# An exponential written in place over the transposed scores in PSUM, in a cross-attention kernel

## The reference, cut to what matters

```python
q = _split_heads(hidden_states @ w_q, HEADS)
out_text = _merge_heads(_sdpa(q, k, v))                      # softmax over 146 text keys
out_ip = _merge_heads(_sdpa(q, k_ip, v_ip, mask=mask_ip))    # softmax over 8 image keys
out = (out_text + IP_SCALE * out_ip) @ w_out + b_out + residual
```

## Time and profile before

| | |
|---|---|
| time, median of 3 runs | 802.34 us (801.8 to 805.32) |
| span of the profiled execution | 801.8 us, as long as the lowest of the runs; no other time is given for it |
| busy TensorE / VectorE / ScalarE / GpSimd | 91% / 71% / 36% / 30% |
| mean granted clock of TensorE | 0.981 |

### The profile page before, as it was taken

The page is one execution under the profiler, slowest core; times in us unless marked ns, Lnnn a source line. Parts: engine busy times, 40 slices in busy tenths (PEclk is TensorE's granted clock), DMA queues, the critical chain, the costliest instruction groups (busy, mean ns, idle before and its releaser), DMA issues.

```text
span 801.8 us, 19010 instructions
## 1 busy us (share of the span) xinstructions
PE 732.8 (91%) x6384; PEld 645.1 (80%) x6384; DVE 565.4 (71%) x1694; ACT 287.3 (36%) x615; POOL 237.1 (30%) x347
## 2 busy tenths in 40 slices
PE   5968979999999999999999899999999999999887
PEld 4755458888888898989898888888898989898766
DVE  3241287778786968687878777786968686878774
ACT  1111026253443525151616152443525151616051
POOL 1000143324150606042423324150606051423334
PEclk9969999999999999999999999999999999999979
DMA  9989714344343525342424344343525342423220
GB/s 257 268 242 220 168 26 109 93 109 112 98 106 86 133 77 129 92 116 80 126 80 118 86 117 108 99 106 85 133 77 131 89 119 80 126 80 93 76 67 34
DMA packets 85115, 91.27 MB, mean 114 GB/s; under 512 B 10768, under 2 KB 69776, under 8 KB 85068
## 3 DMA queue, kind: packets, MB, share of 16 engines
q1 hardware_dynamic: 85084, 90.87, 43.6%
HBM read 40.42 MB, written 10.62 MB: 64 GB/s over the span
## 4 chain that ended last, share of the span: by engine, by line
PE 59%; DVE 18%; SPq 9%; issue 7%; DMA 7%; ACT 1%; DVEq 0%; ACTq 0%
PE psum L864 30%; PE psum L913 7%; PE psum L958 4%; SPq L407 4%; PE psum L939 4%; DVE p_lo L730 4%; PE psum L944 3%; DMA q_stack<-aux_a 3%; DVE o_parts L745 3%; DVE inv_den L737 2%; PE psum L835 2%; DMA q_stack<-mask_scratch 2%; DVE neg_max L706 2%; PE psum L982 2%; PE psum L799 2%
## 5 line engine op out<-in xcount | busy, mean ns | idle before, releaser
L450 POOL TENSOR_TENSOR attn<-o_parts 128x128 f32<-128x128 f32 x160 | 72.9, 456 | 443.0 <-DVE o_parts L742 443.0
L706 DVE TENSOR_REDUCE neg_max<-psum 128x2 f32<-128x292 f32 x320 | 144.1, 451 | 18.0 <-PE psum L913 14.8
L864 PE MATMUL psum<-wo_both,at_hi 128*128 128x320 f32 x640 | 154.1, 313 | 0.0
L730 DVE TENSOR_TENSOR p_lo<-p_whole,p_hi 128x512 f16<-128x512 f32 x160 | 137.1, 857 | 2.4 <-ACT p_hi L553 0.9
L913 PE MATMUL psum<-k_stack,q_stack 104*128 104x154 f32 x640 | 108.5, 284 | 20.0 <-DVE neg_max L707 13.4
L542 ACT ACTIVATE q_hi<-psum 128x256 fp32r<-128x256 f32 x80 | 30.7, 384 | 258.5 <-PE psum L864 258.5
L958 PE MATMUL psum<-v_tail,p_tail 128*128 128x264 f32 x320 | 105.5, 411 | 17.8 <-DVE p_lo L730 15.8
L864 PE MATMUL psum<-xt_hi,wq_hi 128*128 128x256 f32 x400 | 115.2, 288 | 1.0 <-DVE xt_lo L675 1.0
L913 PEld LDWEIGHTS psum<-k_stack,q_stack 104*128 104x128 f32 x640 | 89.6, 193 | 31.3 <-DVE neg_max L707 22.1
L864 PE MATMUL psum<-xt_lo,wq_hi 128*128 128x256 f32 x400 | 113.1, 283 | 0.0
L864 PE MATMUL psum<-xt_hi,wq_lo 128*128 128x256 f32 x400 | 113.0, 283 | 0.0
(11 more groups left out here) (87 smaller groups left out, 1331.4 us busy)
## 6 DMA issues: line engine op xcount, KB each, us to landing
q_stack<-q_hi SPq DMA_DIRECT2D x128, 96.0 KB
x_in<-in_x SPq DMA_DIRECT2D x16, 640.0 KB, 4.1
x_res<-in_x SPq DMA_DIRECT2D x16, 640.0 KB, 4.0
out<-out_sb SPq DMA_DIRECT2D x32, 320.0 KB
q_stack<-q_hi SPq DMA_DIRECT2D x128, 64.0 KB
q_stack<-q_lo SPq DMA_DIRECT2D x64, 96.0 KB
q_stack<-q_lo SPq DMA_DIRECT2D x64, 64.0 KB
q_stack<-aux_a SPq DMA_DIRECT2D x48, 64.0 KB, 2.3
```

What stands on the lines that cost most here:

```text
L450: nc.gpsimd.tensor_tensor(cols, o_parts[:, qt, 0:4, :], o_parts[:, qt, 4:8, :], ALU.add).then_inc(att_half, 1)
L706: nc.vector.tensor_reduce(dst[:, :, 0], src[:, :, 0:TEXT], AX_X, ALU.max, negate=True)
L730: nc.vector.tensor_tensor(p_lo[:, -g % P_SLOTS, 2 * u:2 * u + 2, :], p_whole[:, u, :, :], p_hi[:, -g % P_SLOTS, 2 * u:2 * u + 2, :], ALU.s ...
L864: last = nc.tensor.matmul(ps, l(c), r(c), start=(i == 0), stop=(i == len(terms) - 1))
```

## The change

The buffer `p_whole` goes. ScalarE writes `p_hi` first, and then the full-precision exponential over the scores themselves, in the PSUM bank that it reads. VectorE's split reads that bank. So the bank is in use until the split is done: TensorE's ST step for tile n now waits for the split of tile n-2, where that tile has one (u < 2), and for the exponential where it has none (u = 2). ScalarE's waits for the split go; at the first AT step TensorE waits for the last split. The order of steps on each engine stays as it was, the late place of the splits on VectorE too. In SBUF `at_hi_0` no longer shares its place with other buffers.

```diff
--- before.py
+++ after.py
@@ -227,13 +227,13 @@
         q_stack = sb("q_stack", [P, HEADS, QB], F32R)
         aux_rows = [sb("aux_a", [16 * len(SET_A), QB], F32R), sb("aux_b", [16 * len(SET_B), QB], F32R)]
         p_lo = sb("p_lo", [P, P_SLOTS, 4, QB], F16)
+        at_hi_0 = sb("at_hi_0", [P, QT, 4 * P], F32R)
         with ExitStack() as turns:
 
 
-            at_hi_0, at_lo_0 = (sb(f"at_{part}_0", [P, QT, 4 * P], F32R, turns) for part in ("hi", "lo"))
+            at_lo_0 = sb("at_lo_0", [P, QT, 4 * P], F32R, turns)
             at_hi_1, at_lo_1 = (sb(f"at_{part}_1", [P, QT, P], F32R, turns) for part in ("hi", "lo"))
-            at_hi, at_lo = (at_hi_0, at_hi_1), (at_lo_0, at_lo_1)
-        p_whole = sb("p_whole", [P, 2, 2, QB])
+        at_hi, at_lo = (at_hi_0, at_hi_1), (at_lo_0, at_lo_1)
         p_hi = sb("p_hi", [P, P_SLOTS, 4, QB], F16)
         p_tail = sb("p_tail", [P, P_SLOTS, QB])
         inv_den = sb("inv_den", [P, QT, 8])
@@ -546,20 +546,13 @@
                         act.wait_ge(st_ready, t * 15 - 15 + 3 * g + u + 1)
                         src = scores_t[(3 * g + u) % 2]
                         if u < 2:
-                            if g > 0:
-
-                                act.wait_ge(p_split, t * 10 - 10 + 2 * g + u - 1)
-                            nc.scalar.activation(p_whole[:, u, :, :].rearrange("p h q -> p (h q)"), src[:], ACT.Exp)
                             nc.scalar.activation(p_hi[:, -g % P_SLOTS, 2 * u:2 * u + 2, :].rearrange("p h q -> p (h q)"), src[:],
-                                                 ACT.Exp).then_inc(exp_done, 1)
+                                                 ACT.Exp)
+                            nc.scalar.activation(src[:], src[:], ACT.Exp).then_inc(exp_done, 1)
                         else:
                             nc.scalar.activation(p_tail[:, -g % P_SLOTS, :], src[:, 0:QB], ACT.Exp).then_inc(exp_done, 1)
                     if kind == "AT":
                         qt, u = args
-                        if (qt, u) == (0, 0):
-
-                            act.wait_ge(p_split, t * 10 + 0)
-
                         act.wait_ge(at_ready[u], t * 2 - 2 + qt + 1)
                         c0, c1 = AT_CHUNKS[u]
                         nc.scalar.activation(at_hi[u][:, qt, :], scores_t[u][:, 0:P * (c1 - c0)], ACT.Copy
@@ -727,7 +720,8 @@
                         g, u = args
 
                         dve.wait_ge(exp_done, t * 15 - 15 + 3 * g + u + 1)
-                        nc.vector.tensor_tensor(p_lo[:, -g % P_SLOTS, 2 * u:2 * u + 2, :], p_whole[:, u, :, :],
+                        nc.vector.tensor_tensor(p_lo[:, -g % P_SLOTS, 2 * u:2 * u + 2, :], 
+                                                scores_t[(3 * g + u) % 2][:].rearrange("p (h q) -> p h q", h=2),
                                                 p_hi[:, -g % P_SLOTS, 2 * u:2 * u + 2, :], ALU.subtract).then_inc(p_split, 1)
                     if kind == "PV":
                         g, qt = args
@@ -929,9 +923,13 @@
                             n = 0 if g in SET_A else 1
 
                             pe.wait_ge(aux_in[n], t * (16 * len((SET_A, SET_B)[n])))
-                        if g or u > 1:
-
-                            pe.wait_ge(exp_done, t * 15 - 15 + 3 * g + u - 1)
+                        before = 3 * g + u - 2
+                        if before >= 0 and before % 3 < 2:
+
+                            pe.wait_ge(p_split, t * 10 - 10 + 2 * (before // 3) + before % 3 + 1)
+                        elif before >= 0:
+
+                            pe.wait_ge(exp_done, t * 15 - 15 + before + 1)
                         ps = scores_t[(3 * g + u) % 2]
                         if u < 2:
                             for i in range(2):
@@ -972,6 +970,7 @@
                         if (qt, u) == (0, 0):
 
                             pe.wait_ge(exp_done, t * 15 + 0)
+                            pe.wait_ge(p_split, t * 10 + 0)
                         if qt > 0:
 
                             pe.wait_ge(al_done[u], t * 2 - 2 + qt)
```

## The result

The changed kernel takes 875.46 us (874.18 to 876.49, four runs) against 802.6 us: a ratio of 1.0894, with a 95% interval of 1.0869 to 1.0919. The forecast was 874. The profiled execution spans 872.4 us, 70.6 more than before, where 71.7 were forecast.

A forecast was written before the change was run, and what follows sets the result against it. TensorE's order of work was taken as the bound (busy 91% of 801.8 us). Fifteen blocks at 4.7 us (70.5), plus 3.5 for the BACK-only pass, less 2.3 of DMA waits, made 71.7: 874 us, range 858 to 892.

The forecast's parts named there:

- Durations: VectorE's split from PSUM taken as 0.68 us for all ten in a block, ScalarE's exponential into PSUM as 0.60.
- GpSimd still in the way: Rival: GpSimd still disturbs VectorE's split, which stays at 0.97 us; about 911 us in all, 3%.
- a dearer exponential: Rival: ScalarE's exponential in place takes 0.60 us more; 25 us in all, 880 to 900 us, 12%.
- The block: One full block, TensorE's new waits for splits less what is given back: 4.7 us more, 70.5 for fifteen blocks.
- the 0.2: Near a block's end, AT(0,1) on TensorE waits somewhat longer for `attn`: +0.2 us.
- The sum: Whole kernel: 70.5 + 3.5 - 2.3 = 71.7 us on a span of 801.8, median 0.5 higher: 874 us.
- the last pass: The one pass with BACK alone, no Q step between, partly at half clock: 3.5 us more, bounds 0 and 4.7.
- The three waits for DMAs in the blocks: TensorE's waits for mask-row DMAs before S(0,0) go, since S(0,0) starts 4.5 us later: -2.3 us.
- Faster: Rival: VectorE paces the PV steps, so 0.29 us less on six splits a block gives 786 us; 4%.
- The clock: Rival: TensorE's clock falls in the new waits, 3 us a block, 45 in all, about 920 us; 8%.
- the first rival: The rival of ScalarE's exponential in place costing 0.60 us more: 25 us in all, 900 at the upper bound, 12%.
- The same walk: Step-by-step reckoning of TensorE's waits along one block; with 0.60 us more per in-place exponential, 1.7 more a block.

The follow-up runs named there:

- experiment 4: The kernel before, with GpSimd's additions cut to one column of each head's 32, most attention output left out: 799.95 us, ratio 0.9949.
- experiment 2: The kernel before, SBUF buffer kept, but TensorE's ST steps and first AT step wait for the splits as in the changed kernel: 908.48 us, ratio 1.1301.
- experiment 10: The changed kernel plus a third exponential per tile on ScalarE, written to an unused fp16 buffer between the two: 903.09 us, ratio 1.1268.

## Why the prediction was right, point by point

TensorE's timeline in one block of the changed kernel; its S(4,1) starts at 598.17, that of the block in the earlier trace rows at 553.56, which sets the two side by side:

```profile
602.36 0.39 PE L937 MATMUL psum<-q_stack,k_stack 120*128 120x256 f32 x1 [0.88 <-DVE p_lo L723]
...
607.38 0.39 PE L937 MATMUL psum<-q_stack,k_stack 120*128 120x256 f32 x1 [1.00 <-DVE p_lo L723]
...
610.25 0.39 PE L942 MATMUL psum<-q_stack,k_tail 120*128 120x256 f32 x1 [0.44 <-DVE p_lo L723]
...
611.62 0.39 PE L937 MATMUL psum<-q_stack,k_stack 120*128 120x256 f32 x1 [0.63 <-DVE p_lo L723]
...
614.46 0.39 PE L942 MATMUL psum<-q_stack,k_tail 120*128 120x256 f32 x1 [0.45 <-DVE p_lo L723]
615.83 0.38 PE L937 MATMUL psum<-q_stack,k_stack 120*128 120x256 f32 x1
...
619.58 0.38 PE L942 MATMUL psum<-q_stack,k_tail 120*128 120x256 f32 x1 [1.29 <-DVE p_lo L723]
...
624.43 0.32 PE L907 MATMUL psum<-k_stack,q_stack 104*128 104x154 f32 x1
```

The brackets are the waits that the prediction put there, each behind VectorE's split, at six of the seven ST steps to which it gave a price; at the seventh, ST(4,0), it had only 0.1. The distances from step to step, before and after:

| from, to | before | after | grew | forecast |
|---|---|---|---|---|
| S(4,1), ST(1,0) | 3.02 | 4.19 | 1.17 | 1.2 |
| ST(1,0), ST(2,0) | 4.02 | 5.02 | 1.00 | 1.0 |
| ST(2,0), ST(2,2) | 2.42 | 2.87 | 0.45 | 0.4 |
| ST(2,2), ST(3,0) | 0.55 | 1.37 | 0.82 | 0.8 |
| ST(3,0), ST(3,2) | 2.76 | 2.84 | 0.08 | 0.06 |
| ST(3,2), ST(4,0) | 1.34 | 1.37 | 0.03 | 0.1 |
| ST(4,0), ST(4,2) | 2.28 | 3.75 | 1.47 | 1.4 |
| ST(4,2), S(0,0) | 5.24 | 4.85 | -0.39 | -0.4 |
| S(0,0) to the block's end | | | 0.00 | 0.2 |
| the block | 42.65 | 47.28 | 4.63 | 4.7 |

- *Durations.* The split at 0.68 held (681 ns), and so did the exponential at 0.60 (595). The rivals that hung on them, GpSimd still in the way and a dearer exponential, are out.
- *The block.* The table: every step within 0.1 us but the last, where AT(0,1) did not cost the 0.2. The prediction's own terms add up to 4.76, which it wrote as 4.7; by fifteen blocks that is 0.9 us.
- *The sum.* Fourteen distances between blocks grew by 63.3 us (4.5 each, the lost DMA waits already in it), the last pass by 3.0 (forecast 3.5), the setup by 0.3. The first distance grew by 4.0; it is 53.2 us long before, though the prediction took all fifteen for alike. In all 70.6. The three waits for DMAs in the blocks went, as forecast. In the last step there is some luck: the median stands 3.1 us above the profiled span and not 0.5, and the span is 1.1 us shorter than forecast, so two errors of opposite sign meet in the 874.
- *Faster.* Refuted twice: by the result, and by experiment 4, in which the shorter split alone gave 0.5% and not 2%, as a DMA wait took part of the place of the split's.
- *The clock.* The window from 600 to 620 has TensorE busy 15.32 of 20 us at a granted clock of 1.00. The new waits, 1.3 us at most in this block, did not bring the clock from 2.4 to 1.2 GHz. The prediction put TensorE's share from ST(2,0) to ST(4,2) at 70%; it was 77% (9.39 of 12.20 us). That the rival was worth its place shows in experiment 2: there the clock fell in six full blocks (in the one shown, after a stretch with TensorE busy 70%), for about 5 us in all, not the 45 of the rival.
- *The two rules of the Trainium skill.* That VectorE pays more for a source in PSUM ("VectorE: DVE Perf Modes", the section on the errata) is not borne out: 681 ns from PSUM, 0.69 us from SBUF undisturbed, and the sum without it was the closer one. That idleness takes TensorE's clock back ("TensorE: Matmul & The Clock Gate", Part 1, the HAM clock gate) did not come into play in the changed kernel (clock 1.00 in all fourteen full blocks); the traces of experiments 2 and 10, in which TensorE waits 90.5 and 89.1 us for splits instead of 76.2, agree with it, with 0.97 in six and in five blocks.
- *What the price of the first rival got wrong.* The same walk that gave 25 us for 0.60 us more on each tile gave 17 for 0.49, and experiment 10 measured 27.6. So the upper bound of 900 was too low, but hardly for the reason of too little cover: in blocks at full clock the walk was off by 0.1 to 0.3 us. It left out the clock, which fell in some blocks, and the first block and the last pass, which grew more than the others.

## What to carry to other kernels

Writing a result in place over a PSUM bank lengthens the bank's life to its last reader: ask where that reader stands in its engine's queue, and put its end beside the start of the step that wants the bank next. An order written by hand (here splits two and a half steps late) rests on nobody waiting for what is late; a new wait on it brings in everything that stands ahead in that queue, and moving the reader up gave back 59 of 73 us. And the length of an instruction has no price of its own: 0.16 us less on the split in the mean was worth 3 us where hardly anybody waited for it, and 0.17 us less was worth some 26 us where TensorE did, to which its clock added about 5.

## What I had not expected of the hardware

One ScalarE instruction that reads and writes the same PSUM bank takes 595 ns for 512 columns, no more and no less than into SBUF (595 fp16, 599 fp32), though I had left room for twice that. The split from two operands in SBUF and GpSimd's second addition cost each other in both directions: the split 0.69 to 0.97 us, the addition 454 to 655 ns in the mean. With the split's second source in PSUM both are gone, and GpSimd saves 32 us in an instruction that the change does not touch. GpSimd's first addition (L450), which starts beside the same splits and reads SBUF too, kept its 0.46 us in the kernel before; why it did is not shown. And the granted clock can fall in one block and hold in the next with TensorE busy for the same share of the time (8.70 and 8.66 of 12.5 us, experiment 2), so that blocks of one kernel differ by up to 1.1 us.
